# Decays of seven of eight groups made inside the keys-only steps, with the mask as a TensorE product

## The chip, the cores and the metric

One core of one Trainium2 chip. The metric is the device time of one execution of the kernel, in microseconds. VectorE, ScalarE, GpSimd, TensorE and SyncE (which issues all DMAs here) each run a program of their own, in order, and meet through semaphores.

## The reference

A decoder layer over x of 64 sequences of 64 tokens with 256 features. Three residual parts:

```python
x = x + L0_attn(layernorm(x), ...)      # this is where the change is
x = x + L0_xattn(layernorm(x), ctx, ctx)
x = x + L0_ffn(layernorm(x), ternary(w1), b1, ternary(w2), b2)
```

The first is a gated delta rule with 16 heads. q, k and v come from projections, a causal convolution of four taps and a Silu; q and k are normalised. Two gates per token and head, alpha = sigmoid(x Wa) and beta = sigmoid(x Wb), steer the state:

```python
state = state * alpha
err   = v - state @ k
state = state + beta * outer(k, err)
out   = state @ q
```

The kernel does it without the recurrence: within a sequence, the decay from token s to token t is exp of the sum of log alpha over the tokens between, for s <= t and 0 otherwise. These decays multiply the Gram matrices of keys and queries. The last part uses weights rounded to -1, 0 or 1 by the mean of their absolute values.

## The kernel before

The 64 sequences make G = 8 groups of 8 sequences. A group is 512 tokens, NP = 4 blocks of 128 rows (two sequences each). A unit is one block of one group: 32 in all.

**Opening.** For each group: layer norm (VectorE, with GpSimd for the power), transposes (TensorE), an fp16 high part in XB (ScalarE, L630), a low part (VectorE, `low_parts`), a store of both to XHD, and the gate products (`gates`, TensorE), which `gates_in` (L784) copies to ZG. Between them the projection weights are split into fp16 parts. After the last group the gate arithmetic makes LA, the log of alpha, and BEA, beta.

**Decays.** For each of the 32 units VectorE multiplies a 0/1 pattern by the unit's LA into RHQ (`decay_rows`, L825, 128 x 1024), TensorE multiplies the constant C_LE by it in two fp32 products of 512 columns (L1038), ScalarE takes Exp into EQB (L648), and GpSimd multiplies it with the 0/1 mask C_MQ (L532). Four banks of PSUM serve two units in turn. SyncE stores a whole group at a time, 2 MB, to EQD (L302). In the same stretch VectorE makes the ternary weights W1 and W2.

**Steps.** After that every engine runs `schedule(engine, step)`: first 20 keys-only steps (v is None, k = 0 to 19), and then steps in which the values of head v and the keys of head v + 20 are worked on. A keys-only step does for head k: TensorE two projections (L1053, banks 2 and 3) with the Grams of head k - 1 between them (L1144) and the query sums of head k - 2 (L1092); ScalarE, in this order, the Silu of both results of head k - 1 (L668), a copy of query sums (L694), and for each projection the fourth tap with its bias (L655); VectorE three multiply-adds for each (L864), with the product of Grams and decays between them (L882); GpSimd the squares (L581) and, from step 10, the lane rows (L564, L567) of a batch of 8 heads, which invert a triangular matrix; SyncE a store of the product (`spill`), a load of the decays for head k + 1 (`load_eq`) and a few more.

So in step k VectorE needs the tap of step k (ScalarE), which is queued behind the Silus of head k - 1, of which the second needs the last multiply-add of step k - 1. A wait on several semaphores becomes one that the instruction itself carries and others ahead of it.

The last part of the program is a loop over groups with cross attention and the feed-forward.

## Time and profile before

| | us |
|---|---|
| median of 3 runs | 2951.55 (2937.73 to 2952.56) |
| profiled execution | 2951.72 |
| its span in the profile | 2949.6 |
| TensorE busy | 2376.7 (81%) |
| VectorE busy | 1796.4 (61%) |
| ScalarE busy | 1279.3 (43%) |
| GpSimd busy | 1056.5 (36%) |
| chain that ended last | PE 47%, issue 30%, POOL 7%, SyncE's queue 6%, DVE 5% |

The shares are averages over stages with different limits. PE is TensorE, PEld its weight loads, DVE VectorE, ACT ScalarE, POOL GpSimd, SPq SyncE's queue. PE's clock is told as a share of 2.4 GHz. The span begins with the first instruction, and all times in a profile are from there.

### The profile page before, as it was taken

How to read it: one execution, taken by the hardware profiler on the slowest of the kernel's cores; microseconds unless marked ns; L12 is line 12 of the kernel's file. 1: busy time of each engine (PE TensorE's matmuls, PEld its weight loads, DVE VectorE, ACT ScalarE, POOL GpSimd, SP SyncE). 2: the span in 40 equal slices, each digit the busy share in tenths (PEclk: the TensorE clock that was granted, in tenths of full speed). 3: DMA queues.
4: the chain of work that ended last, by engine and by line, in shares of the span. 5: the costliest groups of instructions: out<-in, count | busy, mean ns of one | idle time of the engine just before them, and what ended most of it. 6: DMA issues, size and time to landing. Idle time of an engine off the chain costs nothing.

```text
span 2949.6 us, 61695 instructions
## 1 busy us (share of the span) xinstructions
PE 2376.7 (81%) x21472; PEld 1487.4 (50%) x21472; DVE 1796.4 (61%) x2860; ACT 1279.3 (43%) x2383; POOL 1056.5 (36%) x1411
## 2 busy tenths in 40 slices
PE   2465569999999999999999999998875656656566
PEld 2222235656666556666565556655543444444345
DVE  5574556676676666667666667644335555555555
ACT  2233335555555555555555555543332323323323
POOL 1392663553653652743734635643000000000000
PEclk9888889999999999999999999999885666656666
DMA  7232233243233233233342342332100000000000
GB/s 265 90 143 107 51 82 80 73 92 85 74 92 80 63 91 89 68 90 79 74 98 77 73 92 76 82 79 55 35 24 26 20 20 20 0 20 20 20 7 7
DMA packets 420560, 200.45 MB, mean 68 GB/s; under 512 B 352784, under 2 KB 374032, under 8 KB 417808
## 3 DMA queue, kind: packets, MB, share of 16 engines
q1 hardware_dynamic: 420240, 196.56, 24.8%
q8 instruction: 155, 2.54, 0.4%
q14 instruction: 165, 1.35, 0.2%
HBM read 124.13 MB, written 72.35 MB: 67 GB/s over the span
## 4 chain that ended last, share of the span: by engine, by line
PE 47%; issue 30%; POOL 7%; SPq 6%; DVE 5%; DMA 3%; ACT 1%; POOLq 0%; DVEq 0%; ACTq 0%
PE PS L1053 18%; PE PS L1066 12%; PE PS L1128 7%; POOL SCR L532 4%; PE PS L1144 3%; PE PS L1101 2%; DVE Y L864 2%; PE PS L1114 2%; DMA SCR<-PGD 1%; PE PS L1085 1%; SPq L351 1%; PE PS L1092 1%; SPq L405 1%; SPq L389 1%; SPq L358 1%
## 5 line engine op out<-in xcount | busy, mean ns | idle before, releaser
L864 DVE SCALAR_TENSOR_TENSOR Y<-PS,CW,Y 128x504 f32<-128x504 f32 (+2 forms) x1536 | 1124.9, 733 | 690.4 <-ACT Y L655 658.5
L655 ACT ACTIVATE Y<-PS,CW 128x512 f32<-128x512 f32 x512 | 398.1, 777 | 634.0 <-PE PS L1053 634.0
L1066 PE MATMUL PS<-WO,XN 128*128 128x256 f32 x2048 | 506.7, 392 | 45.0 <-issue 44.1
L1066 PEld LDWEIGHTS PS<-WO,XN 128*128 128x128 f32 x2048 | 397.1, 195 | 129.8 <-issue 50.1
L1053 PE MATMUL PS<-XK,WH 128*128 128x512 f16 x1024 | 314.1, 389 | 21.3 <-DMA XK<-XHD 20.4
L581 POOL TENSOR_TENSOR SQ<-KQ 128x512 f32<-128x512 f32 x128 | 133.3, 1042 | 528.0 <-PE PS L1092 508.5
L1053 PE MATMUL PS<-XV,WH 128*128 128x512 f16 x1024 | 316.0, 391 | 3.4 <-DMA XV<-XHD 3.4
L680 ACT ACTIVATE XN<-PS,KN 128x256 f32<-128x256 f32 x512 | 215.0, 471 | 172.5 <-PE PS L1066 172.5
L567 POOL TENSOR_TENSOR SCR<-SCR 128x31 f32<-128x31 f32 (+15 forms) x496 | 267.6, 539 | 38.9
L610 POOL TENSOR_TENSOR RSTD<-VE,MHALF 128x4 f32<-128x4 f32 x16 | 16.1, 1008 | 679.5 <-DVE VE L770 679.5
L564 POOL TENSOR_TENSOR SCR<-SCR 128x31 f32<-128x31 f32 (+15 forms) x496 | 242.5, 489 | 42.0 <-issue 9.0
L1128 PE MATMUL PS<-XN,M 64*64 64x256 f32 x2048 | 250.6, 384 | 1.0 <-issue 1.0
L1223 PE MATMUL PS<-CST,SCR 128*128 128x128 f32 x512 | 122.3, 407 | 113.9 <-ACT SCR L740 77.3
L1053 PE MATMUL PS<-XV,WL 128*128 128x512 f16 x512 | 197.9, 386 | 0.0
L1053 PE MATMUL PS<-XK,WL 128*128 128x512 f16 x512 | 197.8, 386 | 0.0
L1128 PEld LDWEIGHTS PS<-XN,M 64*64 64x64 f32 x2048 | 133.2, 133 | 116.2 <-issue 58.5
L941 DVE TENSOR_REDUCE MX<-PS 128x8 f32<-128x512 f32 x128 | 88.6, 692 | 159.4 <-PE PS L1209 149.5
L668 ACT ACTIVATE KQ<-Y 128x512 f32<-128x512 f32 x256 | 159.9, 624 | 45.8 <-DVE Y L864 35.8
L661 ACT ACTIVATE XN<-Y 128x512 f32<-128x512 f32 x256 | 158.5, 619 | 45.6 <-DVE Y L864 45.6
L1223 PEld LDWEIGHTS PS<-CST,SCR 128*128 128x128 f32 x512 | 92.0, 210 | 139.7 <-ACT SCR L736 113.4
L736 ACT ACTIVATE SCR<-SCR 128x512 f32<-128x512 f32 x128 | 80.6, 630 | 186.3 <-DVE SCR L945 186.3
L1144 PE MATMUL PS<-KQ 128*64 128x128 f32 x2048 | 143.0, 283 | 15.9 <-ACT SCR L694 13.2
(118 smaller groups left out, 2985.0 us busy)
## 6 DMA issues: line engine op xcount, KB each, us to landing
PGD<-SCR SPq DMA_DIRECT2D x128, 256.0 KB, 2.1
SCR<-PGD SPq DMA_DIRECT2D x128, 256.0 KB, 3.0
EQD<-SCR SPq DMA_DIRECT2D x8, 2048.0 KB, 6.3
SCR<-EQD SPq DMA_DIRECT2D x128, 128.0 KB, 2.4
SCR<-QND SPq DMA_DIRECT2D x128, 128.0 KB, 3.2
XP<-in_x SPq DMA_DIRECT2D x16, 512.0 KB, 4.6
SCR<-in_wall SPq DMA_DIRECT2D x8, 1024.0 KB, 6.4
SCR<-PGD SPq DMA_DIRECT2D x64, 128.0 KB, 3.4
```

Of the source, the lines that this page charges most:

```text
L564: nc.gpsimd.tensor_tensor(t, LP[:, j, j + 1:BL][:, :, None].broadcast_to([P, n, m]), LY[:, j, 0:m][:, None, :].broadcast_to([P, n, m]), AL ...
L567: nc.gpsimd.tensor_tensor(LY[:, j + 1:BL, 0:m], LY[:, j + 1:BL, 0:m], t, ALU.subtract).then_inc(S["lane"], 1)
L655: A_.activation(Y[:, b, :], PJ[b][:, :], ACT.Identity, scale=CW[:, h[1] % NH, cw0 + 3:cw0 + 4], bias=CW[:, h[1] % NH, cw0 + 4:cw0 + 5]).th ...
L661: A_.activation(V[:, b, :], Y[:, b, :], ACT.Silu).then_inc(S[f"silu{b}"], 1)
L668: A_.activation(KQ[:, k[1] % 2, 3 - b, :], Y[:, b, :], ACT.Silu).then_inc(S[f"silu{b}"], 1)
L680: ins = A_.activation(VW[:, a, :], VWB[:, E * i:E * i + E], ACT.Copy, scale=KN[:, kn, l:l + 1])
L864: V_.scalar_tensor_tensor(yv[:, :, m:T], pv[:, :, 0:T - m], CW[:, h[1] % NH, cw0 + 3 - m:cw0 + 4 - m], yv[:, :, m:T], ALU.mult, ALU.add).t ...
L1053: ins = mm(PJ[b][:, :], wt[:, c, w0:w0 + P], xb[:, xi, :], start=(n == 0), stop=(n == 5))
L1066: ins = mm(VWB[:, E * i:E * i + E], V[:, n, P * a:P * a + P], WO[:, 2 * (w[1] % NH) + n, :], start=(n == 0), stop=(n == 1))
L1128: ins = mm(AC[a // 2][b, E * (a % 2):E * (a % 2) + E], M[b, off % 2, a, :], VW[b, a, :], start=(off % NH == 0 and a % 2 == 0), stop=(off % ...
L1144: ins = mm(gram[64 * n:64 * n + 64, a], KQ[:, s, 0, c0:c0 + 64], KQ[:, s, :, c0:c0 + 64], start=True, stop=True)
L1223: ins = nc.tensor.transpose(PT2[r % 2][:, P * q:P * q + P], ES[:, q // 2, r, 2 * (q % 2):2 * (q % 2) + 2, :], ident)
```

## The change

- Before the steps only the four units of group 0 are made (FIRST = 4). Units 4 to 31 are made at the head of the keys-only steps, one in each of steps 0 to 7, two in each of steps 8 to 17, none in 18 and 19: VectorE's row product, TensorE's products, ScalarE's two Exp, SyncE's store.
- The mask is no longer a GpSimd product. RHQ and C_LE swap the roles of strict and non-strict comparison, and TensorE adds the identity times MASKN in fp16, which is 0 where s <= t and -500 elsewhere, so that Exp gives 0.
- All units use banks 0 and 1; TensorE counts once a unit (dec_mm), as does ScalarE (dec_exp), and TensorE waits for the Exp of the unit before.
- EQD is stored unit by unit, 512 KB, in pieces of 256 bytes; in a step this stands ahead of spill and load_eq. RHQ lies in XB, EQB in XN, LA in M.
- The ternary weights are made in halves of 1024 columns in steps 3, 5, 17 and 19, w1 first; w2 is loaded a second time in step 11.
- In the opening `gates_in` runs one group later, and a gate product takes alpha and beta together (32 columns, 24 products a group for 48 of 16). XB loses its pad column.

The diff, cut to its core:

```diff
-        EQB = [scr(4096 * i, 4096).rearrange("p (h a t) -> p h a t", h=NH, a=NP) for i in range(2)]
-        RHQ = [V.rearrange("p a (h t) -> p (a h) t", t=T), VW.rearrange("p a (h t) -> p (a h) t", t=T)]
+        EQB = [XN[:, i].rearrange("p a e -> p (a e)").rearrange("p (h t) -> p h t", t=T) for i in range(2)]
+        RHQ = [XB[:, i].rearrange("p c t -> p (c t)").bitcast(F32).rearrange("p (h t) -> p h t", t=T) for i in range(2)]
...
+        UNITS = G * NP
+        FIRST = NP
+        AT_STEP = [1] * 8 + [2] * 10 + [0, 0]
+        def units_of(v, k):
+            if v is not None:
+                return range(0)
+            n0 = FIRST + sum(AT_STEP[:k[1]])
+            return range(n0, n0 + AT_STEP[k[1]])
...
# SyncE
-            for g in range(G):
-                s = g % 2
-                sp.wait_ge(S["masked"], at(8 * g + 8))
-                sp.dma_start(EQD[g].rearrange("p h x -> p (h x)"), scr(4096 * s, 4096)).then_inc(S[f"st_eq{s}"], 16)
+            def store_eq(n):
+                g, p, s = n // NP, n % NP, n % 2
+                sp.wait_ge(S["dec_exp"], at(n + 1))
+                sp.dma_start(EQD[g].rearrange("p h (a t) -> p h a t", t=T)[:, :, p, :], EQB[s]).then_inc(S[f"st_eq{s}"], 16)
...
+            stored_eq(NP)
             sp.dma_start(XK[:, :, :], XHD[0]).then_inc(S["ld_xk"], 16)
...
+                for n in units_of(v, k):
+                    store_eq(n)
# GpSimd
-                        nc.gpsimd.tensor_tensor(eq, eq, CST[:, C_MQ:C_MQ + 64][:, None, :].broadcast_to([P, 8, T]), ALU.mult).then_inc(S["masked"], 1)
# ScalarE
+            def exponents(n):
+                s = n % 2
+                act.wait_ge(S["dec_mm"], at(n + 1))
+                if n >= 2:
+                    act.wait_ge(S[f"st_eq{s}"], at(16 * (n // 2)))
+                for i in range(2):
+                    ins = A_.activation(EQB[s][:, 8 * i:8 * i + 8, :], PJ[i][:, :].rearrange("p (h t) -> p h t", h=8), ACT.Exp)
+                ins.then_inc(S["dec_exp"], 1)
...
             def step(v, k):
                 w, kp, kq = (None if v is None else back(v)), back(k), back(k, 2)
+                for n in units_of(v, k):
+                    exponents(n)
...
# VectorE
-                if g:
-                    gates_in(g - 1)
+                if g >= 2:
+                    gates_in(g - 2)
...
+            def decay_rows(n):
+                if n >= 2:
+                    dve.wait_ge(S["dec_mm"], at(n - 1))
+                V_.tensor_tensor(RHQ[n % 2], CST[:, C_MQ:C_MQ + 64][:, None, :].broadcast_to([P, NH, T]),
                                  LA[:, n, :][:, :, None].broadcast_to([P, NH, T]), ALU.mult).then_inc(S["rhq_done"], 1)
...
             def step(v, k):
+                for n in units_of(v, k):
+                    decay_rows(n)
+                if v is None:
+                    if k[1] == 2:
+                        ternary_scales()
+                    if k[1] in (3, 5):
+                        ternary(0, k[1] // 4)
+                    if k[1] in (17, 19):
+                        ternary(1, k[1] // 18)
# TensorE
+            def decays(n):
+                pe.wait_ge(S["rhq_done"], at(n + 1))
+                pe.wait_ge(S["dec_exp"], at(n))
+                for i in range(2):
+                    mm(PJ[i][:, :], CST[:, C_LE:C_LE + 128], RHQ[n % 2][:, 8 * i:8 * i + 8, :].rearrange("p a t -> p (a t)"),
+                       start=True, stop=False)
+                    ins = mm(PJ[i][:, :], IDH[:, :], MASKN[:, :, :].rearrange("p h t -> p (h t)"), start=False, stop=True)
+                ins.then_inc(S["dec_mm"], 1)
...
             def step(v, k):
+                for n in units_of(v, k):
+                    decays(n)
```

## Rows read from the trace of the kernel before

**Rows 1.** Windows by stage: stretch, its length, busy time by engine, clock, DMA
```profile
103.62:244.76 141.14, 76.25 (x129) 29.14 (x129) 78.43 (x43) 37.53 (x65) 109.79 (x65) 0.79 0.31 128
244.76:392.86 148.10, 88.97 (x642) 40.67 (x644) 88.05 (x126) 52.73 (x91) 66.13 (x90) 0.88 0.22 59
```

**Rows 2.** Timeline of VectorE in the opening: start, length, line, idle before
```profile
33.51 0.29 DVE L784 COPY XV<-PS 128x128 f32<-128x128 f32 x1 [3.33 <-PE PS L1020]
...
43.83 0.29 DVE L784 COPY XV<-PS 128x128 f32<-128x128 f32 x1 [3.33 <-PE PS L1020]
...
82.33 1.41 DVE L762 BATCH_NORM_STATS2 STT<-XP 128x6 f32<-128x256 f32 x4 [5.04 <-DMA XP<-in_x]
...
95.49 0.29 DVE L784 COPY XV<-PS 128x128 f32<-128x128 f32 x1 [1.54 <-PE PS L1020]
```

**Rows 3.** Single lines of the decays: ns min/median/max, first and last start
```profile
L825 DVE TENSOR_TENSOR XN<-CST,XK x32: 1216/2078/2333, 103.6 to 214.0; 128x1024 f32<-128x1024 f32 x32
...
L532 POOL TENSOR_TENSOR SCR<-SCR,CST x64: 1252/1266/3308, 124.8 to 232.0; 128x512 f32<-128x512 f32 x64
```

**Rows 4.** Timeline of ScalarE, in the decays and in a keys-only step
```profile
98.11 1.28 ACT L638 ACT_TABLE_LOAD   x1
99.69 0.63 ACT L638 ACTIVATE Y<-Y 128x512 f32<-128x512 f32 x1 [0.30 <-DVE Y L813]
107.06 1.28 ACT L648 ACT_TABLE_LOAD   x1 [6.74 <-PE PS L1038]
...
110.98 0.60 ACT L648 ACTIVATE SCR<-PS 128x512 f32<-128x512 f32 x1 [0.26 <-PE PS L1038]
...
391.36 0.63 ACT L668 ACTIVATE KQ<-Y 128x512 f32<-128x512 f32 x1 [1.90 <-DVE Y L864]
...
392.05 0.77 ACT L655 ACTIVATE Y<-PS,CW 128x512 f32<-128x512 f32 x1
```

**Rows 5.** Who waited for whom, 248 to 412: total, times, longest
```profile
PE PS L1092 <- POOL SQ L581: 43.8, 7, 13.1
```

**Rows 6.** Timeline of TensorE's products in the keys-only steps
```profile
244.76 1.01 PE L1053 MATMUL PS<-XK,WH 128*128 128x512 f16 x2 [20.43 <-DMA XK<-XHD]
...
344.76 0.65 PE L1092 MATMUL PS<-SQ,ONES 128*32 128x128 f32 x8 [5.02 <-POOL SQ L581]
```

**Rows 7.** Timeline of VectorE from the last decays into the keys-only steps
```profile
239.81 1.03 DVE L854 MEMSET SCR<- 128x512 f32 x2 [23.52 <-DMA EQD<-SCR]
248.33 4.68 DVE L864 SCALAR_TENSOR_TENSOR Y<-PS,CW,Y 128x504 f32<-128x504 f32 x6 [7.49 <-ACT Y L655]
...
260.97 2.27 DVE L864 SCALAR_TENSOR_TENSOR Y<-PS,CW,Y 128x504 f32<-128x504 f32 x3 [1.53 <-ACT Y L655]
...
263.76 2.26 DVE L864 SCALAR_TENSOR_TENSOR Y<-PS,CW,Y 128x504 f32<-128x504 f32 x3
267.55 2.27 DVE L864 SCALAR_TENSOR_TENSOR Y<-PS,CW,Y 128x504 f32<-128x504 f32 x3 [1.53 <-ACT Y L655]
...
386.27 2.27 DVE L864 SCALAR_TENSOR_TENSOR Y<-PS,CW,Y 128x504 f32<-128x504 f32 x3 [1.53 <-ACT Y L655]
...
392.86 2.27 DVE L864 SCALAR_TENSOR_TENSOR Y<-PS,CW,Y 128x504 f32<-128x504 f32 x3 [1.53 <-ACT Y L655]
```

**Rows 8.** DMA issues by line: count, KB of each, median us to landing
```profile
EQD<-SCR SPq DMA_DIRECT2D x8, 2048.0 KB, 6.3
...
XP<-in_x SPq DMA_DIRECT2D x16, 512.0 KB, 4.6
...
XHD<-XB SPq DMA_DIRECT2D x8, 512.0 KB, 3.5
```

**Rows 9.** Timeline of TensorE's weight loads in the decays: start, length, idle before
```profile
117.78 0.50 PEld L1038 LDWEIGHTS PS<-XN,CST 128*128 128x128 f32 x2 [4.23 <-DVE XN L825]
...
119.66 0.34 PEld L1038 LDWEIGHTS PS<-XN,CST 128*128 128x128 f32 x1 [0.52 <-issue]
...
123.62 0.19 PEld L1038 LDWEIGHTS PS<-XN,CST 128*128 128x128 f32 x1 [0.24 <-issue]
```

More of the change, by code:

```diff
@@ L250, in after, with begins @@
             return not isinstance(h[0], int) or h[0] * NH + h[1] >= n
+        UNITS = G * NP
[6 more added lines that the diff above has]
+            return range(n0, n0 + AT_STEP[k[1]])
+        def begins(v):
+            return v is not None and isinstance(v[0], int) and v[0] * NH + v[1] == 0
         def schedule(eng, step):
@@ L426, in keep, with stored_eq @@
                 sp.dma_start(X1D[ds(g, 1)].rearrange("o p n e -> (o p) n e"), XP[:, 0]).then_inc(S["st_x1"], 16)
+            def stored_eq(units):
+                for s in range(2):
+                    sp.wait_ge(S[f"st_eq{s}"], at(8 * units))
             sp.wait_ge(S["zero_e"], at(2))
+            stored_eq(NP)
             sp.dma_start(XK[:, :, :], XHD[0]).then_inc(S["ld_xk"], 16)
@@ L439, in step @@
                     sp.nop(nofuse=True)
+                if v is None and k[1] == NH - 1:
+                    stored_eq(2 * NP)
+                if v is None and k[1] == 11:
+                    sp.wait_ge(S["tern_done"], 7)
+                    sp.dma_start(WRAW[1], w2).then_inc(S["ld_tern2"], 16)
                 if v is None and k[1] == NH + AHEAD - 1:
+                    stored_eq(UNITS)
                     load_values((0, 0))
@@ L451, in step @@
                         residual(v[0] + v[1] // NH)
+                if begins(v):
+                    sp.wait_ge(S["tern_done"], 11)
+                for n in units_of(v, k):
+                    store_eq(n)
                 if exists(back(k, 1)):
@@ L638, in _ @@
             A_.activation(LTA, GEX[:, 0], ACT.Ln).then_inc(S["gate_s"], 1)
[L640 to L649 removed]
+            def exponents(n):
[6 more added lines that the diff above has]
+                ins.then_inc(S["dec_exp"], 1)
+            for n in range(FIRST):
+                exponents(n)
             def tap(h, b):
@@ L697, in step @@
                 w, kp, kq = (None if v is None else back(v)), back(k), back(k, 2)
+                for n in units_of(v, k):
+                    exponents(n)
+                if begins(v):
+                    for s in range(2):
+                        act.wait_ge(S[f"st_eq{s}"], at(8 * UNITS))
                 if exists(kp):
@@ L819, in _ @@
             dve.wait_ge(S["gate_v"], at(5))
-            def decay_rows(g, p):
-                n = NP * g + p
+            for s in range(2):
+                dve.wait_ge(S[f"st_xh{s}"], at(64))
+            def decay_rows(n):
                 if n >= 2:
-                    dve.wait_ge(S["dec_mm"], at(2 * n - 2))
-                V_.tensor_tensor(RHQ[p % 2], CST[:, C_UTC:C_UTC + 64][:, None, :].broadcast_to([P, NH, T]),
+                    dve.wait_ge(S["dec_mm"], at(n - 1))
+                V_.tensor_tensor(RHQ[n % 2], CST[:, C_MQ:C_MQ + 64][:, None, :].broadcast_to([P, NH, T]),
@@ L826, in decay_rows @@
                                  LA[:, n, :][:, :, None].broadcast_to([P, NH, T]), ALU.mult).then_inc(S["rhq_done"], 1)
[L828 to L829 removed]
+            for n in range(FIRST):
+                decay_rows(n)
+            for u in range(2):
+                V_.memset(EN[u], 0.0).then_inc(S["zero_e"], 1)
             dve.wait_ge(S["ld_tern"], 32)
             for n in range(2):
[L832 removed]
@@ new lines, in ternary @@
+            def ternary(n, half):
+                dst = (W1[:, :, :].rearrange("p c f -> p (c f)"), W2[:, :, :].rearrange("p f e -> p (f e)"))[n]
+                cols = slice(1024 * half, 1024 * half + 1024)
+                m = 3 + 4 * n + 2 * half
+                if n:
+                    dve.wait_ge(S["ld_tern2"], 16)
+                dve.wait_ge(S["tern_done"], m)
+                V_.tensor_scalar(TERN, WRAW[1][:, cols], SMALL[:, 6 + n:7 + n], None, ALU.is_lt).then_inc(S["tern_done"], 1)
+                dve.wait_ge(S["tern_done"], m + 1)
+                V_.scalar_tensor_tensor(dst[:, cols], WRAW[1][:, cols], SMALL[:, n:n + 1], TERN, ALU.is_gt, ALU.subtract).then_inc(S["tern_done"], 1)
@@ L1029, in _ @@
             gates(G - 1)
-            for g in range(G):
-                for p in range(NP):
-                    n0 = NP * g + p
-                    pe.wait_ge(S["rhq_done"], at(n0 + 1))
-                    if n0 >= 2:
-                        pe.wait_ge(S["dec_exp"], at(2 * n0 - 2))
-                    for n in range(2):
-                        mm(PJ[2 * (p % 2) + n][:, :], CST[:, C_LE:C_LE + 128], RHQ[p % 2][:, 8 * n:8 * n + 8, :].rearrange("p a t -> p (a t)"),
-                           start=True, stop=True).then_inc(S["dec_mm"], 1)
+            def decays(n):
[6 more added lines that the diff above has]
+                ins.then_inc(S["dec_mm"], 1)
+            for n in range(FIRST):
+                decays(n)
             pe.wait_ge(S["w_split"], 8)
@@ L1147, in step @@
             def step(v, k):
+                for n in units_of(v, k):
+                    decays(n)
+                if begins(v):
+                    pe.wait_ge(S["dec_exp"], at(UNITS))
                 w = None if v is None else back(v)
```

105 lines of the change are left out of this document (38 added, 67 removed).

## The prediction, made before the change was run

> **What bounds the kernel now.** I read the busy time by stages first [rows 1]. The change touches the first 392.86 us; what follows belongs to code that it leaves alone but for a few waits long met. Of the three stretches, the opening is 103.62 us. The decays take 141.14 us, and there GpSimd is the busiest engine (109.8 us) while TensorE is busy 76.3 and ScalarE 37.5. The first 18 keys-only steps take 148.10 us with no engine over 89 us busy.
>
> Next, in the opening, VectorE's timeline [rows 2]: one group is 10.32 us (33.51 to 43.83), of which VectorE stands 3.33 us before it can copy the gates of the group before; the last group also waits 5.04 us for its x.
>
> Then the decays, line by line [rows 3]. 64 GpSimd masks at a median of 1.27 us, and the row product on VectorE has a median of 2.08 us where its minimum is 1.22. The masks start from 124.8 to 232.0, the last store lands and VectorE clears EN at 239.81, the first key product starts at 244.76 [rows 6, 7]. So from the first row product (103.6) to the first convolution of step 0 (248.33) pass 144.7 us.
>
> Last, a keys-only step [rows 7]. From one first convolution to the next are 6.58 us (260.97 to 267.55). VectorE's work is 5.05 of it (260.97 to 266.02), and 1.53 pass on ScalarE, which has to do the second Silu, the query sums and the tap in turn [rows 4]. It is a ring VectorE, ScalarE, VectorE without slack. Seventeen steps take 137.94 us (248.33 to 386.27), 26 us more than 17 times 6.58: TensorE waited 43.8 us in all for the squares queued behind GpSimd's lane rows [rows 5]. Step 18 comes 6.59 later.
>
> **What the change removes.** All 64 masks, and 28 of 32 units from the serial stretch. Four units stay. The first: a row product without GpSimd beside it 1.25, TensorE 4.27 (below), hand-off 0.4, two Exp 1.05 = 7.0. The next three can't overlap, as all share two banks and one count: 2.14 at the full clock + 0.4 + 1.05 = 3.6 each, 10.8. Then the last unit's store: nearest rows are 3.5 us for 512 KB and 6.3 for 2048 KB [rows 8]; its pieces are 256 bytes, so I take 5.0. The load of XK and its hand-over take 4.0 (244.76 less 239.81, less the two EN memsets' 1.03, which now run earlier), and from the first key product to the first convolution 3.57 remain. Sum 30.4 in place of 144.7: 114.3 saved. Bounds: 103 (all units at the lower clock, a slow store) to 117.
>
> Opening. Gates are copied one group later, which takes the 3.33 wait away [rows 2]. A group is then 7.0 us on VectorE, but its x is asked for some 3.9 us into the group two before the one that needs it and takes 4.6 [rows 8], so 8.5 is the new pace. The wait of the last group for x is behind 5 MB of weights that are asked for one pace earlier per group; I take 6.3 for all groups. After it 3.33 more, and 0.7 of the 1.54 us in which VectorE waits for the last gates [rows 2], as these have 24 products of 32 columns for 48 of 16. Together 10.3; bounds 4 and 16. The two new constants cost about 0.5, in that figure.
>
> The final XN/XB moves, LA in M and the unpadded XB cost nothing: they change addresses alone. The stores of XHD must have landed before the first row product; the last one is issued before the 8 us of gate arithmetic and takes 3.5 [rows 8], so it is hidden.
>
> **What the change adds.** Unit 4 belongs to step 0 and runs while XK is loaded: free, its cover is the 9 us of store and load. Steps 1 to 7 carry one unit each, steps 8 to 17 two. On every engine the unit stands at the head of the step. VectorE starts the row product when the last convolution of step k-1 is done; TensorE needs it; ScalarE waits for TensorE with both Silus and the tap queued behind; and VectorE's next convolution waits for that tap. So the unit is inserted whole into the ring. Its terms:
>
> Row product 1.25 (minimum in rows 3, with a hand-off). Where GpSimd works on lane rows beside it I take the median, 2.1 [rows 3], in six steps: about 1 more each.
>
> TensorE: two fp32 products of two passes and two fp16 products, each 512 columns. TensorE has stood some 4.4 us by then (tap, three convolutions, row product). In the decays, after 4.23 us of standing at 117.78, the passes came every 0.86 us (0.34 + 0.52, at 119.66), which is 1.2 GHz, and by 123.62, 5.8 us after the restart, every 0.43, 2.4 GHz [rows 9]; after 5.02 us at 344.76 the products also ran at the lower clock [rows 6]. So 4 x 0.853 + 2 x 0.427 = 4.27, at the full clock 2.14. I take 4.15.
>
> Hand-off 0.4, two Exp 1.05 (0.60 each, overlapped) [rows 4].
>
> Table loads. Exp and Silu are not served by one table here: 1.28 us each time [rows 4]. Each step with units now needs Exp's and then Silu's. Which side of a wait a load falls on differs: the one at 98.11 ran ahead of its ACTIVATE, which only began at 99.69; the one at 107.06 began only after the product had ended. The latter ACTIVATE names another wait first and dec_mm second; the changed one names dec_mm first. I take it that Exp's load is then done while TensorE works, at nothing (its cover is 4.15 us; 16 x 1.28 = 20.5 us if it isn't), and that Silu's load, 1.3, is on the path in all 17 steps.
>
> The Trainium skill ("ScalarE: Activation LUTs", What ACT_TABLE_LOAD costs, and the rule under Table sets: The hidden batching unit to batch calls by set) speaks against this change, and gives 2.66 us for a switch with its drain. The trace shows the 1.28 and no drain beside it (98.11 + 1.28 = 99.39, next start 99.69 by its input); by the page's figure, an estimate, the 17 switches on the path would cost 23 us more.
>
> The first Silu, now behind the unit: 0.54. Grams and the second projection after a further pause at TensorE: 0.3, between nothing and 1.6 at the lower clock.
>
> One-unit step: 6.58 + 1.25 + 4.15 + 0.4 + 1.05 + 1.3 + 0.54 + 0.3 = 15.6. A second unit can't start before the Exp of the first; its row product is ready and the table stays: TensorE 2.9 (2.14 full, 4.27 low; the pause is only 1.5 us, so nearer the full clock) + 0.4 + 1.05 = 4.35, the step 19.95. Total 7 x 15.6 + 10 x 19.95 + 6 = 314.7, for 137.9 before: 176.8 more. GpSimd's lane rows are by then shorter than a step, so the 26 us of waiting are gone, and that is in the figure.
>
> Hidden: the ternary halves and scales (VectorE, behind the row products while TensorE and ScalarE work on the unit, or in step 19 in which VectorE waits anyway); the second load of w2; store_eq at the head of SP's step, where spill and load_eq behind it need a later product of VectorE. A unit waits for the store of the unit two before, a step old. If the store took over 12 us it would show.
>
> **Sum.** 176.8 - 114.3 - 10.3 = +52 us. On the profiled execution (2951.72, its span 2949.6, 2.1 around it; the median of the runs is 2951.55) this gives 3004.
>
> **Rivals.**
> (a) Both loads on the path and TensorE mostly at the lower clock: +20.5, second units at 4.27 (+14), grams and projection 17 x 0.7 (+12): 3050, from 3032 up. For: 107.06. Against: 98.11 and the short pauses.
> (b) TensorE stays at 2.4 GHz through the steps: in place of 4.15 comes 2.14 (17 x 2.0 = 34), second units save 7.6, grams 5, the first units 2: 49 less, 2955, which is no slower than before. The point from which it decides: the 17 intervals must average under 15.4 us ((137.9 + 114.3 + 10.3)/17). In the steady steps before, with pauses of some 1.1 us, the clock was full; against it are 4.23 and 5.02 us of standing, both followed by the lower clock [rows 6, 9]. The Trainium skill ("TensorE: Matmul & The Clock Gate", Part 1) also has the clock fall in idleness and rise after sustained work, and by that rule, the trace agrees.
> (c) The unit is hidden: ScalarE or TensorE has the products ready before the convolutions end, and only the two stretches' savings stay: 2951.7 - 124.6 + 17 x 1.3 = 2849. The order within every queue rules it out as I read it.
>
> **Chances.** My case 0.62, (a) 0.20, (b) 0.12, (c) 0.04, a shortfall of the opening or stores the rest, within my case's range. Likeliest case alone: 2983 to 3025 (a half of TensorE's 34 us, the opening's bounds). The range for 8 in 10: 2966 to 3048. A run of this kernel can tell about 0.5% from no change (14.8 us). Slower by more 0.84, within it 0.09, faster 0.07.
>
> **What would show it.** Convolution starts in steps 1 to 7 some 15.6 apart, in 8 to 17 some 20; the first key product near 121; 33 more table loads, those for Exp while TensorE works; weight loads of 0.34 in most first units; masks gone and row products at 1.2 us; EQD stores of 512 KB at 4 to 6 us. After step 18 both kernels should keep pace. The prediction is wrong if steps are near 13 (clock full), near 17 and 22 (both loads on the path), or if Silus run before the Exps.

## The result, and the profile after

The changed kernel takes 2978.65 us (median of 4 runs, 2973.37 to 2981.83) where the kernel before takes 2949.31 (4 runs beside it). The ratio is 1.0105, with a 95% interval from 1.0072 to 1.0138: 1.05% slower. The profiled execution is 2981.19 us, its span 2979.3, which is 29.7 us longer than the span before. The forecast was 3004 us, or +52; the measured median lies below the prediction's likeliest range (2983 to 3025) and inside its wider one (2966 to 3048).

I first cut the span at the first row product, at the first convolutions of step 0 and step 17, and at the end. The prediction's seventeen intervals lie between these two convolutions; the second stretch of [rows 1] goes one step further. The columns are those of [rows 1].

```profile
0.00:88.79 88.79, 21.02 (x256) 19.37 (x256) 61.58 (x147) 29.57 (x30) 10.35 (x18) 1.00 0.73 268
88.79:118.37 29.58, 17.77 (x39) 6.31 (x40) 11.24 (x9) 6.21 (x11) 1.26 (x1) 0.89 0.58 142
118.37:423.23 304.86, 183.91 (x755) 72.33 (x754) 121.83 (x154) 118.39 (x171) 73.52 (x90) 0.80 0.34 76
423.23:2979.30 2556.07, 2188.41 (x20300) 1392.79 (x20296) 1576.01 (x2556) 1163.54 (x2203) 869.70 (x1238) 0.88 0.24 59
```

No engine is busy for more than 184 of its 305 us: the steps are a chain of waits. TensorE's granted clock there is 0.80 of 2.4 GHz, a mean over the two levels; it was 0.88 in the keys-only steps before [rows 1].

VectorE's timeline gives the cuts themselves; it answers to [rows 2] and [rows 7].

```profile
31.72 1.41 DVE L796 BATCH_NORM_STATS2 STT<-XP 128x6 f32<-128x256 f32 x4 [0.97 <-DMA XP<-in_x]
...
39.77 1.41 DVE L796 BATCH_NORM_STATS2 STT<-XP 128x6 f32<-128x256 f32 x4 [1.05 <-DMA XP<-in_x]
...
71.56 1.40 DVE L796 BATCH_NORM_STATS2 STT<-XP 128x6 f32<-128x256 f32 x4 [8.64 <-DMA XP<-in_x]
...
80.66 0.29 DVE L818 COPY XV<-PS 128x128 f32<-128x128 f32 x1 [0.72 <-PE PS L1065]
...
88.79 2.36 DVE L863 TENSOR_TENSOR XB<-CST,M 128x1024 f32<-128x1024 f32 x2
...
118.37 4.45 DVE L902 SCALAR_TENSOR_TENSOR Y<-PS,CW,Y 128x504 f32<-128x504 f32 x6 [12.21 <-ACT Y L682]
...
164.68 2.27 DVE L902 SCALAR_TENSOR_TENSOR Y<-PS,CW,Y 128x504 f32<-128x504 f32 x3 [6.63 <-ACT Y L682]
...
169.65 1.22 DVE L863 TENSOR_TENSOR XB<-CST,M 128x1024 f32<-128x1024 f32 x1
180.01 2.27 DVE L902 SCALAR_TENSOR_TENSOR Y<-PS,CW,Y 128x504 f32<-128x504 f32 x3 [9.14 <-ACT Y L682]
...
224.62 2.27 DVE L902 SCALAR_TENSOR_TENSOR Y<-PS,CW,Y 128x504 f32<-128x504 f32 x3 [9.14 <-ACT Y L682]
...
423.23 2.27 DVE L902 SCALAR_TENSOR_TENSOR Y<-PS,CW,Y 128x504 f32<-128x504 f32 x3 [9.67 <-ACT Y L682]
```

Groups of the opening now start 8.05 us apart (31.72 to 39.77), each with about a microsecond of waiting for x, for 10.32 before; the last group stands 8.64 for its x (71.56), where it stood 5.04 [rows 2]. A keys-only step with one unit is 15.33 (164.68 to 180.01), and VectorE stands 9.14 of it in front of its convolution; before, it stood 1.53 [rows 7]. What it waits for is ScalarE's tap (L682), and why the tap is late stands on ScalarE's timeline of the same step:

```profile
166.57 0.78 ACT L682 ACTIVATE Y<-PS,CW 128x512 f32<-128x512 f32 x1 [1.92 <-PE PS L1099]
167.36 1.28 ACT L672 ACT_TABLE_LOAD   x1
175.59 1.08 ACT L672 ACTIVATE XN<-PS 128x512 f32<-128x512 f32 x2 [6.95 <-PE PS L1082]
176.70 1.28 ACT L695 ACT_TABLE_LOAD   x1
177.99 1.15 ACT L695 ACTIVATE KQ<-Y 128x512 f32<-128x512 f32 x2
179.05 0.26 ACT L721 ACTIVATE SCR<-PS 128x128 f32<-128x128 f32 x1
179.20 0.77 ACT L682 ACTIVATE Y<-PS,CW 128x512 f32<-128x512 f32 x1
```

Read it from the top. Exp's table load follows the last tap at once (167.36). Then ScalarE stands 6.95 us in front of Exp (L672). Only behind Exp and Silu's table load come the Silus (177.99), the query sums and the tap that VectorE needs. The step adds up as 4.97 of VectorE (164.68 to 169.65), 5.94 for the row product, TensorE and their hand-offs (to 175.59), 1.11 for two Exp, 1.29 for the load, and 2.02 for Silus, query sums and tap (177.99 to 180.01): 15.33.

TensorE's weight loads in steps with two units show what the clock does.

```profile
236.18 0.30 PEld L1080 LDWEIGHTS PS<-XB,CST 128*128 128x128 f32 x2 [2.57 <-issue]
...
249.28 0.50 PEld L1080 LDWEIGHTS PS<-XB,CST 128*128 128x128 f32 x2 [4.88 <-DVE XB L863]
250.29 0.15 PEld L1082 LDWEIGHTS PS<-MASKN,IDH 128*128 128x128 f16 x1 [0.52 <-issue]
251.15 0.76 PEld L1080 LDWEIGHTS PS<-XB,CST 128*128 128x128 f32 x2 [0.70 <-issue]
...
255.15 0.50 PEld L1080 LDWEIGHTS PS<-XB,CST 128*128 128x128 f32 x2 [2.57 <-issue]
```

After 4.88 us of standing a pair of fp32 loads takes 0.50 us, as in the 1.2 GHz start of [rows 9], and the second unit of that step (255.15) has the same 0.50. At the full clock such a pair takes 0.30 (236.18, the second unit of the step before). The length of the pause alone doesn't tell the level: of the first units of steps 1 to 8, three (at 156.12, 186.25 and 230.85) begin with a pair of 0.30 or 0.31 after the same 4.89 us. On ScalarE the distance from the first unit's Exp to the second's is 3.65 us in one step and 5.43 in the next (over the ten steps with two units, six times 3.65 or 3.66 and four times 5.19 to 5.43, 4.31 on the mean):

```profile
234.98 1.08 ACT L672 ACTIVATE XN<-PS 128x512 f32<-128x512 f32 x2 [6.40 <-PE PS L1082]
238.63 1.09 ACT L672 ACTIVATE XN<-PS 128x512 f32<-128x512 f32 x2 [2.57 <-PE PS L1082]
...
253.95 1.09 ACT L672 ACTIVATE XN<-PS 128x512 f32<-128x512 f32 x2 [6.94 <-PE PS L1082]
259.38 1.08 ACT L672 ACTIVATE XN<-PS 128x512 f32<-128x512 f32 x2 [4.34 <-PE PS L1082]
```

Last, single lines and DMA issues, which answer to [rows 3] and [rows 8]. The steps hold 33 table loads: 16 for Exp (a seventeenth, at 85.5, is the opening's) and 17 for Silu.

```profile
L863 DVE TENSOR_TENSOR XB<-CST,M x32: 1214/1216/1620, 88.8 to 410.4; 128x1024 f32<-128x1024 f32 x32
...
L672 ACT ACT_TABLE_LOAD  x17: 1283/1283/1283, 85.5 to 407.0; - x17
...
L695 ACT ACT_TABLE_LOAD  x17: 1283/1283/1283, 129.8 to 419.9; - x17
...
EQD<-XN SPq DMA_DIRECT2D x32, 512.0 KB, 4.1
```

The masks on GpSimd are gone. With them went most of the row product's slowdown: its median is 1.216 us, where it was 2.078 [rows 3]. In e4_upfront below, where all 32 row products run up front as before but without masks, none takes over 1.23.

### The profile page after: what moved, and what is told of

Same layout as the page of the kernel before. It is cut to its first block, busy times and chain, and to the rows that moved or that the text cites. A ratio compares the mean times of both kernels' runs of the same rounds, so it can differ in the third digit from the quotient of the medians.

```text
span 2979.3 us, 61463 instructions
## 1 busy us (share of the span) xinstructions
PE 2411.1 (81%) x21344; PEld 1490.8 (50%) x21344; DVE 1770.7 (59%) x2865; ACT 1317.7 (44%) x2415; POOL 954.8 (32%) x1347
## 4 chain that ended last, share of the span: by engine, by line
PE 49%; issue 31%; SPq 6%; DVE 6%; DMA 3%; ACT 3%; POOL 2%; POOLq 0%; DVEq 0%; ACTq 0%
PE PS L1099 17%; PE PS L1112 11%; PE PS L1174 7%; PE PS L1080 3%; DVE Y L902 3%; PE PS L1190 3%; PE PS L1147 2%; PE PS L1160 2%; DMA SCR<-PGD 1%; SPq L369 1%; SPq L423 1%; DMA XP<-in_x 1%; PE PS L1131 1%; SPq L407 1%; PE PS L1138 1%
## 5 line engine op out<-in xcount | busy, mean ns | idle before, releaser
L682 ACT ACTIVATE Y<-PS,CW 128x512 f32<-128x512 f32 x512 | 398.0, 777 | 610.3 <-PE PS L1099 610.3
L593 POOL TENSOR_TENSOR SCR<-SCR 128x31 f32<-128x31 f32 (+15 forms) x496 | 270.9, 546 | 38.9
L590 POOL TENSOR_TENSOR SCR<-SCR 128x31 f32<-128x31 f32 (+15 forms) x496 | 246.1, 496 | 33.0
L1273 PE MATMUL PS<-CST,SCR 128*128 128x128 f32 x512 | 121.8, 405 | 115.1 <-ACT SCR L772 78.0
L1080 PE MATMUL PS<-XB,CST 128*128 128x512 f32 x128 | 104.9, 915 | 102.1 <-DVE XB L863 86.9
L695 ACT ACTIVATE KQ<-Y 128x512 f32<-128x512 f32 x256 | 158.0, 623 | 15.2 <-issue 10.0
```

Source lines behind the costliest of these rows:

```text
L590: nc.gpsimd.tensor_tensor(t, LP[:, j, j + 1:BL][:, :, None].broadcast_to([P, n, m]), LY[:, j, 0:m][:, None, :].broadcast_to([P, n, m]), AL ...
L593: nc.gpsimd.tensor_tensor(LY[:, j + 1:BL, 0:m], LY[:, j + 1:BL, 0:m], t, ALU.subtract).then_inc(S["lane"], 1)
L682: A_.activation(Y[:, b, :], PJ[b][:, :], ACT.Identity, scale=CW[:, h[1] % NH, cw0 + 3:cw0 + 4], bias=CW[:, h[1] % NH, cw0 + 4:cw0 + 5]).th ...
L695: A_.activation(KQ[:, k[1] % 2, 3 - b, :], Y[:, b, :], ACT.Silu).then_inc(S[f"silu{b}"], 1)
L1080: mm(PJ[i][:, :], CST[:, C_LE:C_LE + 128], RHQ[n % 2][:, 8 * i:8 * i + 8, :].rearrange("p a t -> p (a t)"), start=True, stop=False)
```

## The experiments

One marker serves for all kernels: VectorE's product with the Grams (TENSOR_TENSOR SCR<-PS,SCR), of which each keys-only step from step 1 on has one. In the table, "start" is the time from the first row product to the product of step 1. The two "mean step" columns are the means of the intervals from step 1 to 7 (six; one unit each in the changed kernel) and from 7 to 17 (ten; two units each). In e3_late, e5, e6 and e11 the units stand at the end of a step, so these intervals hold those of the step before: for e3, e5 and e6 the second column has nine steps with two units and one with one, and the units of step 17 fall behind it. "Rest" is from step 19 to the end. All are us, worked out from VectorE's timeline.

| kernel | opening | start | mean step, 1 to 7 | mean step, 7 to 17 | 1 to 17 | 17 to 19 | rest | span |
|---|---|---|---|---|---|---|---|---|
| before | 103.62 | 152.95 | 6.58 | 9.24 | 131.89 | 25.74 | 2535.4 | 2949.6 |
| after | 88.79 | 46.33 | 15.28 | 19.86 | 290.30 | 23.64 | 2530.2 | 2979.3 |
| e1_warm | 90.55 | 43.24 | 13.36 | 17.13 | 251.48 | 23.55 | 2526.1 | 2934.9 |
| e2_no_exp | 90.17 | 46.18 | 14.04 | 17.12 | 255.38 | 24.95 | 2519.4 | 2936.1 |
| e9_wait_order | 89.68 | 46.27 | 17.58 | 22.01 | 325.56 | 25.14 | 2531.2 | 3017.9 |
| e3_late | 89.14 | 40.49 | 10.07 | 13.37 | 194.17 | 23.08 | 2520.7 | 2867.6 |
| e4_upfront | 88.40 | 140.56 | 6.70 | 9.38 | 133.98 | 25.24 | 2522.9 | 2911.1 |
| e8_gates_now | 98.90 | 45.90 | 15.24 | 19.84 | 289.84 | 23.69 | 2522.9 | 2981.2 |
| e7_pack4 | 89.83 | 63.56 | 23.84 | 9.42 | 237.25 | 25.84 | 2522.3 | 2938.8 |
| e5_late_banks | 88.62 | 36.51 | 10.09 | 11.52 | 175.76 | 27.40 | 2521.6 | 2849.9 |
| e10_upfront_banks | 91.25 | 109.53 | 6.70 | 9.36 | 133.83 | 26.45 | 2521.1 | 2882.2 |
| e6_late_banks_warm | 88.70 | 38.37 | 8.46 | 11.43 | 165.01 | 25.65 | 2523.0 | 2840.7 |
| e11_two_each | 89.07 | 40.06 | 10.61 | 10.82 | 171.82 | 24.87 | 2527.6 | 2853.4 |

"Rest" runs through code that is the same in all of them and still spreads over 16 us; no theory here is read from that column. e3, e4, e5, e6 and e11 have four executions each, beside seven of the kernel before; the others have one execution each and are read by their steps.

**e1_warm: what the clock costs.** TensorE gets work without a purpose behind its last projection of a step, so that it doesn't stand before the unit.

```
                if exists(k):
                    project(k, 3, XK, "ld_xk")
+               if v is None and k[1] < 17:
+                   for _ in range(16):
+                       mm(AC[0][:, :], IDH[:, :], MASKN[:, :, :].rearrange("p h t -> p (h t)"), start=True, stop=True)
```

> The changed kernel with 16 more fp16 products of 512 columns at the end of TensorE's step 0 to 16, into a bank that nothing reads there; they fill some 3.4 us of the pause before each unit. Theory (the clock's part): in the changed kernel the first unit of a step takes 4.27 us at 1.2 GHz; kept busy, TensorE stays at 2.4 GHz, the unit takes 2.14 and the 17 intervals shrink by about 2 us each, 34 us in all, to some 2945. Rival (the clock costs nothing, because the ring is set by ScalarE and VectorE): no change, 2979. A second rival: the products delay the unit itself, then up to 3 us more a step.

The steps from 1 to 17 are 38.8 us shorter (34 expected), a one-unit step 1.9, a two-unit step 2.7. The one execution took 2936.70 us. TensorE's weight loads (first the ones without a purpose, then the unit's) show the fp32 passes at the full clock:

```profile
159.28 3.34 PEld L1225 LDWEIGHTS PS<-MASKN,IDH 128*128 128x128 f16 x16
...
164.05 0.30 PEld L1080 LDWEIGHTS PS<-XB,CST 128*128 128x128 f32 x2 [1.43 <-DVE XB L863]
...
165.01 0.41 PEld L1080 LDWEIGHTS PS<-XB,CST 128*128 128x128 f32 x2 [0.33 <-issue]
```

The pause before the unit is 1.43 us where it was 4.9, and the mean clock of this stretch is 0.98 where it was 0.80. So the lower clock was 39 of the 158 us by which these steps had grown.

**e2_no_exp: what the table costs.** Units 4 to 31 are evacuated by a Copy in place of Exp; this kernel leaves the exponential out, and with it all table loads of the steps but one for Silu (131.02).

```
+                   if n < FIRST:
+                       ins = A_.activation(EQB[s][:, 8 * i:8 * i + 8, :], src, ACT.Exp)
+                   else:
+                       ins = A_.activation(EQB[s][:, 8 * i:8 * i + 8, :], src, ACT.Copy, scale=0.0)
```

> The changed kernel with the Exp of units 4 to 31 replaced by a Copy with scale 0, so the exponential is left out in the steps and no table has to be switched there; everything else stays. Theory (the ring, with one load on the path): steps with a unit shrink by the Silu load alone, 1.3 us x 17 = 22 us, to some 2957; a one-unit step from 15.2 to 13.9. Rival (table switching is what the change costs: both loads, with a drain): 17 x 5.3 = 90 us less, 2889. Rival (the loads are hidden): no change.

A one-unit step falls by 1.24 us on the mean, as expected. A two-unit step falls by 2.7, which is more than one load, so the steps from 1 to 17 are 34.9 us shorter for 22 expected (2938.01 us in one execution for 2957). ScalarE's timeline has the Copy and then Silu with nothing between; TensorE's weight load of a second unit is at the full clock there:

```profile
160.60 1.09 ACT L676 ACTIVATE XN<-PS 128x512 f32<-128x512 f32 x2 [8.24 <-PE PS L1086]
161.57 1.15 ACT L699 ACTIVATE KQ<-Y 128x512 f32<-128x512 f32 x2
```

```profile
247.20 0.30 PEld L1084 LDWEIGHTS PS<-XB,CST 128*128 128x128 f32 x2 [2.57 <-issue]
```

The mean clock of the steps rose from 0.80 to 0.84. The rows suggest that a gain of TensorE, more of whose work is at the full clock, comes on top of the load's; no run took the two apart.

**e9_wait_order: which load is hidden.** ScalarE's two waits before Exp change places, the store first and then TensorE.

```
-                act.wait_ge(S["dec_mm"], at(n + 1))
                 if n >= 2:
                     act.wait_ge(S[f"st_eq{s}"], at(16 * (n // 2)))
+                act.wait_ge(S["dec_mm"], at(n + 1))
```

> The changed kernel with the two waits ahead of the Exp of a unit named in the other order, the store first and dec_mm second. The same waits and instructions. Theory (the wait named first is carried by the ACTIVATE, the others stand ahead of it, and the table load goes between them): Exp's load now starts only when TensorE has finished the unit, 1.28 us more in each of 16 steps, 20 us in all: 3000 or some 16.5 us for a one-unit step. Rival (the place of the load doesn't hang on that order): 2979, 15.2.

```profile
164.76 1.28 ACT L672 ACT_TABLE_LOAD   x1 [7.88 <-PE PS L1082]
166.05 1.09 ACT L672 ACTIVATE XN<-PS 128x512 f32<-128x512 f32 x2
```

Now the load stands behind the wait for TensorE (7.88) and Exp starts right after it. The steps are 35.3 us longer, 2.2 per step, for the 20 that the load alone would add; the one execution took 3019.72 us for 3000 expected. Part of the rest is clock again: the mean falls to 0.77, and in the one-unit steps VectorE now waits before its second convolution too, for the tap of a projection that ran at the lower level; in the changed kernel it doesn't from step 2 to 7.

```profile
156.91 2.27 DVE L902 SCALAR_TENSOR_TENSOR Y<-PS,CW,Y 128x504 f32<-128x504 f32 x3 [1.97 <-ACT Y L682]
```

The same rule is seen where nothing was exchanged: in e6_late_banks_warm below, with TensorE's wait named first, one of Exp's loads (292.76) stands 0.21 us for the store, whose wait is named second.

**e3_late: where in the step the unit stands.** TensorE's, ScalarE's and SyncE's part of the unit move from the head of the step to its end. VectorE's row product stays at the head.

```
             def step(v, k):
-                for n in units_of(v, k):
-                    exponents(n)
...
                 if exists(k):
                     tap(k, 3)
+                for n in units_of(v, k):
+                    exponents(n)
```

> The changed kernel with the unit's TensorE products, its two Exp and its store moved from the head to the end of each step; the row product stays at the head. The same instructions, in another order. Theory (what costs is the place at the head of the step, where the Silus and the tap queue behind the unit and VectorE behind them): products and Exp then run beside the convolutions. A one-unit step takes 9 to 11 us for 15.2, a two-unit step 12 to 15 for 19.9; 2979 falls to 2860 to 2900, clearly faster than before. Rival (the engines are short of time, the unit's work itself is the cost): two-unit steps stay near 20 us and the time within 20 us of 2979.

This is the largest effect: 96.1 us less from step 1 to 17, and 2875.51 us against 2940.78 for the kernel before, a ratio of 0.9783 (0.9767 to 0.9799). It holds the same units, loads and products as the changed kernel. Of the 96.1 us almost nothing is moved into the next interval with the units of step 17: from 17 to 19 it takes 23.08 for 23.64. ScalarE's timeline:

```profile
161.17 0.78 ACT L682 ACTIVATE Y<-PS,CW 128x512 f32<-128x512 f32 x1 [3.55 <-PE PS L1099]
161.96 1.28 ACT L672 ACT_TABLE_LOAD   x1
163.32 1.08 ACT L672 ACTIVATE XN<-PS 128x512 f32<-128x512 f32 x2
164.42 1.28 ACT L695 ACT_TABLE_LOAD   x1
165.71 1.15 ACT L695 ACTIVATE KQ<-Y 128x512 f32<-128x512 f32 x2
```

Exp has no wait in front of it in this one-unit step: the unit was done while the taps were being made. Both table loads are on the ring now, and the step is still 5.2 us shorter. The wait of 6.95 in front of Exp was most of the cost, and not the load of Exp's table.

**e4_upfront: the other parts of the change alone.** All 32 units are made before the steps, with `FIRST = UNITS` and `AT_STEP = [0] * 20`; the masks by product, the opening and the moved buffers stay.

> The changed kernel with all 32 units made before the steps, one after the other as its first four are; no unit in the steps. It separates the mask as a TensorE product (with the new opening) from the move into the steps. Theory: a unit up front costs 3.65 us, the pace of the first four, so 28 of them add 102 us before the first key product, and the steps are as in the kernel before (137.9 us from step 0 to step 17 for 304.9): 2979 + 102 - 167 = 2914, faster than before by 35. Rival (the stores in 256-byte pieces, 512 KB each, can't follow at that pace, or move the bound to the DMA queues): a unit takes 4.5 to 6 us and the time is 2940 to 2980.

2912.83 us, a ratio of 0.9914 (0.9897 to 0.9931). The opening gains 15.2 and the serial decays 12.4; the steps are as before (+2.1). So the change had a half that helps by itself, by 0.9%. Moving 28 units into the head of the steps gave back 94.2 in the start and lost 156.3 from step 1 to 17.

**e8_gates_now: what the opening owes to the later copy.** The gates are copied one group after they are made, as before.

```
-                if g >= 2:
-                    gates_in(g - 2)
                 if g:
+                    gates_in(g - 1)
                     n = g - 1
```

> The changed kernel with the gates copied in the same group again, as before, everything else as changed. It undoes the opening's one reordering. Theory: VectorE waits again for TensorE in each group, 2.5 us for the 3.3 before (the gate products are half as many), a group takes 9.5 us for 8.0 in the changed kernel, and the first row product starts at 99 to 102 us for 88.8: 10 to 13 us of the 14.8 gained there. Rival (the gain is that of the fewer gate products, or the load of x sets the pace in either case): 88 to 93 us.

The first row product moves from 88.79 to 98.90: 10.1 of the 14.8 us come from this reordering, a little less certain than it looks, as the kernels with the changed opening start their first row product anywhere from 88.40 to 91.25. The whole time doesn't show it (2983.02 us in one execution, 4.4 above the changed kernel's median), because the rest is 7.3 shorter in this execution. VectorE's timeline has groups 9.70 apart again, with the wait for TensorE back:

```profile
31.21 0.29 DVE L818 COPY XV<-PS 128x128 f32<-128x128 f32 x1 [2.71 <-PE PS L1063]
...
40.91 0.29 DVE L818 COPY XV<-PS 128x128 f32<-128x128 f32 x1 [2.70 <-PE PS L1063]
```

**e7_pack4: is the cost one of units or of steps?** `AT_STEP = [4] * 7 + [0] * 13`.

> The changed kernel with four units in each of steps 0 to 6 and none later; order and instructions as in the changed kernel. Theory (a step that carries units pays some 8.6 us once, for the first unit, the load of Silu's table and the first Silu, and 3.7 to 5.4 for each further unit): steps 1 to 6 take 15.2 + 3 x (3.7 to 5.4) = 26 to 31 us, the rest are as in the kernel before, with its waits for GpSimd's lane rows; step 1 to 17 takes 255 to 290 us for 290, the time is 2950 to 2985. Rival (the cost is by unit, 28 of them, wherever they are): 290 us and more, as the 26 us of waits for GpSimd come back on top: 3000 or more.

Steps with four units are 26.3 to 28.1 us; the first six intervals hold five of them and one without any. The first unit of a step costs 8.7 (15.28 less 6.58), each further one about 4. From step 1 to 17 that is 53 us less than in the changed kernel, and 40.5 in the span. The total of 237.25 lies below the 255 to 290 expected, and the 2940.55 us below 2950 to 2985: the theory's own terms, 26 to 31 us for the five such steps in these intervals and the rest as before, add up to 229 to 254 only. The last ten intervals have 9.42 on the mean: TensorE's waits for GpSimd's lane rows came back there, 31.1 us of them up to step 17 and 13.2 behind it, 44.4 in all for the 43.8 of [rows 5].

**e5_late_banks: the second unit of a step.** e3, and each unit has its own pair of banks, so that TensorE can make the second one while ScalarE takes the first.

```
+        DB = [PJ[0:2], AC]
...
-                pe.wait_ge(S["dec_exp"], at(n))
+                if n >= 2:
+                    pe.wait_ge(S["dec_exp"], at(n - 1))
                 for i in range(2):
-                    mm(PJ[i][:, :], CST[:, C_LE:C_LE + 128], ...
+                    mm(DB[n % 2][i][:, :], CST[:, C_LE:C_LE + 128], ...
```

> e3_late with a second pair of banks (6 and 7, idle until values begin) for odd units, so that TensorE need not wait for the Exp of the unit before. In e3_late a two-unit step took 13.73 us and a one-unit step 10.07, 3.66 more, which is the pace of serial units (2.14 on TensorE, 0.4, 1.09 on ScalarE). Theory (the second unit costs what is serial in it): now it costs 1.1 to 2.2, a two-unit step 11.2 to 12.3, one-unit steps stay at 10.1; 15 to 25 us less in the ten steps and some 4 in the first four units: 2850 to 2858 for e3_late's 2875. Rival (the store of the unit two before, or VectorE's row product, holds the second unit): two-unit steps stay above 13.

2853.8 us, ratio 0.9697 (0.9676 to 0.9719). One-unit steps stay at 10.08; eight of nine two-unit steps fall from 13.73 to between 10.58 and 12.28. The ninth takes 15.10: TensorE stands 4.77 us in front of the query sums (227.42) until the squares, queued behind GpSimd's lane rows, end at 227.32. The longer steps of e3 and of the changed kernel had no such wait before step 17.

**e10_upfront_banks: the banks without the steps.** e4 with the same banks.

> e4_upfront with the second pair of banks. e4_upfront took 3.65 us a unit, serial through TensorE, the hand-off and ScalarE. Theory: with two pairs TensorE sets the pace, 2.14 a unit, 28 units take 40 us less: 2870 to 2885. Rival (two buffers for Exp's results and a store of 4.1 us with its issue and hand-over bind at some 2.9 to 3.3 a unit): 2895 to 2905. In either case more than the 2841 of e6_late_banks_warm, as the units still stand in front of the steps.

2883.97 us; 31.0 less in the start than e4. ScalarE's timeline says what bounds a unit now:

```profile
118.80 1.08 ACT L673 ACTIVATE XN<-PS 128x512 f32<-128x512 f32 x2 [1.92 <-DMA EQD<-XN]
121.13 1.09 ACT L673 ACTIVATE XN<-PS 128x512 f32<-128x512 f32 x2 [1.25 <-DMA EQD<-XN]
```

Exp waits for the store of the unit two before, and starts 2.33 and 3.03 us apart in turn, 2.7 on the mean. The time came out as the theory had it (2870 to 2885), the mechanism as the rival had it, though at a quicker pace than the rival's 2.9 to 3.3.

**e6_late_banks_warm: the clock in the better order.** e5, with eight products without a purpose between a step's first projection (bank 2) and the Grams. The expectation numbers the two projections by their banks, 2 and 3, as "second" and "third".

```
                if exists(k):
                    project(k, 2, XK, "ld_xk")
+               if v is None:
+                   for _ in range(8):
+                       mm(VWB[:, :], IDH[:, :], MASKN[:, :, :].rearrange("p h t -> p (h t)"), start=True, stop=True)
```

> e5_late_banks with eight more fp16 products of 512 columns between the second projection and the Grams of each keys-only step, into a bank that nothing reads there; they fill the 2 us in which TensorE waits for the Silus. In e3_late the Grams and the third projection that follow this pause run partly at 1.2 GHz (products 0.43 us apart), and VectorE waits 1.45 us for that tap. Theory (the ring has become ScalarE, Grams, projection, tap, and the clock is in it): one-unit steps fall from 10.1 to 8.6 to 9.2, two-unit steps by 0.5 to 1.5, 15 to 25 us in all. Rival: the ring is ScalarE's own work (two loads, Exp, Silus), then nothing changes.

2841.27 us, ratio 0.9652 (0.9629 to 0.9674), the best of all. One-unit steps are 8.44. The Grams and the second projection (bank 3) stand on the ring between the Silus and the second tap. TensorE's timeline, e6 first and e5 second:

```profile
158.10 1.09 PE L1192 MATMUL PS<-KQ 128*64 128x128 f32 x16 [0.32 <-ACT SCR L722]
159.13 0.60 PE L1101 MATMUL PS<-XK,WH 128*128 128x512 f16 x2
```

```profile
172.77 1.09 PE L1192 MATMUL PS<-KQ 128*64 128x128 f32 x16 [2.04 <-ACT SCR L722]
173.79 1.03 PE L1101 MATMUL PS<-XK,WH 128*128 128x512 f16 x2
```

The Grams take 1.09 in both of these steps (in other steps of e5 up to 1.80), but behind a pause of 2.04 the projection's pair of products takes 1.03 and behind one of 0.32 it takes 0.60. VectorE's wait for the second tap, 0.93 to 1.55 us in e5 up to step 8, is gone, and the granted clock of the steps is 0.98 for 0.89.

Over all, 12.5 us were gained for 15 to 25 expected. The seven one-unit steps gave 11.5 of it. The nine two-unit steps gave nothing (11.67 us on the mean in e5, 11.76 in e6), with single intervals of 15.21 and 13.31 among many of 10.59. In these TensorE stands 5.11 and 2.26 us in front of the query sums (216.51 and 273.48). The timeline names no releaser there, but GpSimd's squares end 0.1 us earlier (216.41 and 273.38): its lane rows, which the squares queue behind, are longer than the step again.

**e11_two_each: an even load.** e6 with two units in each of the first 14 steps.

> e6_late_banks_warm with two units in each of steps 0 to 13 and none later. There a one-unit step took 8.44 us and a two-unit step 10.59, apart from those that wait for GpSimd's lane rows, and a step without a unit 6.58. Theory (the first unit of a step costs 1.9, a second 2.15, so that packing saves little): steps 1 to 13 take 10.6 each and the last four 6.6 to 12 with the lane rows' waits: within 5 us of 2841. Rival (fewer steps with two table loads save 4 x 2.6 us): 2830.

2855.65 us, a ratio of 0.9712 (0.9696 to 0.9728) and 14 more than e6; both theories missed. Most steps with two units are at 10.59, one is at 16.08 and one at 12.30. TensorE's timeline in front of the query sums, the last such wait up to step 17, e11 first and e6 second:

```profile
285.92 0.65 PE L1140 MATMUL PS<-SQ,ONES 128*32 128x128 f32 x8 [4.93 <-POOL SQ L608]
```

```profile
273.48 0.43 PE L1140 MATMUL PS<-SQ,ONES 128*32 128x128 f32 x8 [2.26 <-issue]
```

From step 1 to 17 e11 takes 6.8 us more. Without any wait e6 would have 154.4 there (7 x 8.44 + 9 x 10.59) and e11 157.4 (13 x 10.59 + 3 x 6.58), so 3.0 of it is the other spread of the units. Up to step 17 TensorE stands in front of the query sums for 11.3 us in e11 (5.11, 1.24, 4.93) and for 8.5 in e6 (5.11, 1.09, 2.26), which is 2.8 more. What else separates the two, in the start and the rest, is not explained.

## Why the prediction was right, point by point

The forecast had the sign and the way right, and put the loss at 52 us where it was 29.7, below the likeliest range that it gave. Every line of the table below came out on the fast side of its term. By its own terms (in the prediction's convolutions, so step 1 to 7 means seven intervals, 118.37 to 224.62):

| term | predicted | measured |
|---|---|---|
| opening | -10.3 | -14.8 |
| decays and start | -114.3 | -115.1 (144.7 to 29.6) |
| steps 0 to 17 | +176.8 | +166.9 (137.9 to 304.9) |
| steps 17 to 19 | 0 | -2.1 |
| rest | 0 | -5.2 |

**The unit is inserted whole into the ring: shown.** e3 moves nothing but the unit's place and takes 96 us away. Rival (c), the hidden unit, is out in this order.

**Steps 1 to 7, 15.6 predicted, 15.18 measured.** Row product, TensorE and hand-off were put at 5.80 and took 5.94 in the step shown; Exp 1.05 and 1.11; Silu's load 1.3 and 1.29. Over all 17 intervals the time from a row product's start to Exp's is 5.16 to 6.33, 5.79 on the mean, with the low end where a part of the unit ran at the full clock. The 0.3 for Grams and second projection was not there in this step: from the first Silu to the convolution pass 2.02, which is 1.53 plus the 0.54 of the Silu less 0.05. But as a mean over the 17 intervals it was right: in steps 1, 15 and 16 Grams and second projection ran at the lower level, and VectorE stood 1.55, 1.45 and 1.45 before its second convolution, 4.45 us in all for the 5.1 that 17 x 0.3 makes. VectorE's timeline, step 15:

```profile
386.52 2.27 DVE L902 SCALAR_TENSOR_TENSOR Y<-PS,CW,Y 128x504 f32<-128x504 f32 x3 [1.45 <-ACT Y L682]
```

**Steps 8 to 17, 19.95 and 0.6 predicted, 19.86 measured.** The mean of the second unit was right (4.35 predicted, 4.31 measured), its picture wasn't, and that is luck: I took one value between the two levels, and the trace has six steps at 3.65 and four at 5.19 to 5.43. The contended row products, taken at 2.1 from a stretch where GpSimd made masks, were at most 1.62 beside its lane rows. Only a step's first row product stands on the ring, and just two of these were slowed, to 1.61 and 1.28 (330.43 and 349.80), 0.5 us in all for the 6 in the sum. That is the term that was mis-sized most, 5.5 of the 9.9 us by which the steps were put too long: the same engine beside it, but not the same instructions.

**GpSimd's lane rows: right.** The steps grew longer than the lane rows, and up to step 17 TensorE no longer waits for the squares; the one such wait left is behind it (442.69, 9.51 us). Of the 43.8 us that the prediction set beside its 26, 13.1 were behind step 17 too (at 407.83), so the 30.7 before it are what goes with the 26.

**Table loads: right, on both sides.** e9 shows that Exp's load is hidden only by the order of the two waits, e2 that a one-unit step without Silu's is 1.24 us shorter; in a two-unit step e2 saved 2.7, of which the load explains 1.28. The Trainium skill ("ScalarE: Activation LUTs", What ACT_TABLE_LOAD costs) gives 2.66 us for a switch with a drain of the engine; here the load is 1.283 us and the next instruction starts 0.01 us behind it, so the measured number decides.

**Clock: rival (b) was a size, not a case.** The fall of the clock in the unit came in most steps as foretold [rows 9], and e1 prices it: 38.8 us from step 1 to 17, for 49 less when TensorE never falls. With e1's steps the kernel is at the time of before (2936.7 us in one run, beside 2940.78), as rival (b) has it. Rival (a) wanted both loads on the path and more of the lower clock; e9 put both loads on the path, and with the granted clock at 0.77 its run took 3019.7, less than the 3032 at which that rival began.

**Opening: mis-sized.** Up to the x of the last group the prediction took 6.3 us off, and that x came 10.8 earlier (71.56 for 82.33). Behind it 4.06 were saved (21.29 us to the first row product before, 17.23 now) for 4.03, mostly the 3.33 and the last wait for gates, which fell from 1.54 to 0.72. So the 4.5 us lie where the prediction let the weights and the last x be asked for earlier. The pace of the groups was 8.05 for 8.5, but that isn't the whole of it, as VectorE then stood 8.64 for the last x; why this landed when it did was not taken apart. e8 puts 10.1 of the 14.8 on the later copy; what the other 4.7 owe to fewer gate columns or to the earlier weights stays open too.

**Decays and start: right.** The units after the first come 3.65 us apart for 3.6, the store took 4.1 for 5.0. The first key product was at 114.78; by the terms it stood at 120.2 (93.3 + 30.4 - 3.57). Of these 5.4 us the opening has 4.5, the store the rest.

**Rest: open.** The -7.3 behind step 17 is inside what kernels with the same code there differ by (the rests above span 16 us), and the kernel before alone ran from 2937.73 to 2952.56 us, with the profiled execution near the top. The forecast's error, 22.5 us, is 9.9 of the steps, 7.3 of this, 4.5 of the opening and 0.8 of the start.

## What to carry to other kernels

Work that is moved into a chain without slack costs its whole latency wherever it stands in front of what the chain waits for. Place it behind the chain's last hand-over on each in-order engine, and have its inputs made earlier in the step: the same instructions cost 156 us at the head of these steps (over e4, which has no unit in them) and 60 at their end. Before splitting a stage over many steps, count what is paid per step and not per item (a restart of TensorE, a table switch, the first hand-off), and give consecutive items separate banks. Look at which wait an instruction names first, and at what the chain's engines do while they stand.

## What the runs showed of the hardware that was not expected

- Two waits in a row before an ACTIVATE are not alike. With TensorE's wait named first, the table load ran before it was met (167.36, Exp at 175.59); with the store's first, behind it (164.76, Exp at 166.05). The exchange cost 35 us in its one run.
- Small savings and small costs grew in this chain. Taking 1.28 us out of a two-unit step took 2.7, and adding 1.28 to a step added 2.2 on the mean, with the granted clock at 0.84 and 0.77 for 0.80.
- Products that compute nothing paid for themselves: 16 per step, 3.34 us of weight loads, made a step of 15.28 us one of 13.36. The Trainium skill ("TensorE: Matmul & The Clock Gate", Part 1) has the clock rise with sustained work; the clock of 0.98 in e1's steps agrees.
- Beside GpSimd's masks VectorE's row product had a median of 2.08 us, beside its lane rows and squares never more than 1.62 in the changed kernel and 2.04 in e6_late_banks_warm, and without GpSimd beside it 1.22.
